# A language-model block on one core: projections a full step further ahead of the scores, a fifth buffer of values, and one buffer for the rests of q and k

## The chip, the core and the metric

The kernel runs on one core of one Trainium2 chip. The metric is the device time of one execution in microseconds (us), lower is better. The kernel before takes 623.44 us (median of three executions, 623.02 to 623.56).

## The reference

4096 tokens (32 rows of 128) of width 256 are looked up in a table, pass through causal attention with 16 heads of width 16, and then through a top-1 mixture of 8 experts (256 to 1024 to 256, GELU) with a capacity per expert. Each half takes a normalised input and is added to `h`.

```python
h = take(L0_tok_weight, x, axis=0)                       # (32, 128, 256)
n = layernorm(h)
q, k, v = (einsum('hkd,bsd->bhsk', w, n) for w in (q_w, k_w, v_w))
scores = where(causal, einsum('bhqk,bhsk->bhqs', q, k) / 4, -inf)
h = h + einsum('hdv,bhsv->bsd', o_w, einsum('bhqs,bhsk->bhqk', softmax(scores), v))
n = layernorm(h)
probs = softmax(n @ wg);  top1 = argmax(probs)           # 8 experts, slots in order of tokens
y = gelu(slots_of(n) @ W1 + b1) @ W2 + b2                # erf GELU
h = h + where(valid, y[slot], 0) * probs[top1]
```

## The kernel before

`attention_phase` handles the 32 rows in 16 groups of two (`NG` = 16, `GB` = 2); `expert_phase` then handles the 8 experts one after the other, bound by TensorE all along. The change touches the attention phase alone.

Attention is written as one loop of steps (line 257) that every engine runs through in its own queue, in order; semaphores alone tie the queues together. Each step `i` is cut into 8 places `s` (0 to 7). In step `i` a group `g = i` is projected: TensorE turns the normalised rows `xn` (line 767), ScalarE copies them as `xth`, VectorE makes the low part `xtl`, TensorE projects q at place 1, k at place 2 and v at place 7 (line 570, 12 matmuls of 256 columns for each). `turn4(bM0, xn)` for the next group stands at place 7 too.

Scores are needed with float32 accuracy from bfloat16 matmuls, so q and k are each split in three bfloat16 parts. For q: ScalarE writes the first part (`first_part`, line 456), VectorE the rest `qr` (`rest_of`, line 810), ScalarE the second part (line 461), GpSimd the third from `qr` (line 407). The same follows for k, with `kr` and line 410. The SP queue writes the parts to memory (lines 309 and 312) and reads them back stacked by head (`stacks`, line 301) into `qs` and `ks`, which have four buffers (`RING` = 4).

The scores, whose order is set by the three lags at line 267, come in 8 units for each group. A first pass (S, lines 599 and 602) only gives maxima (VectorE, `maxima`, line 796; a unit of TensorE waits for the maxima of the unit two before, as there are two banks). The maxima are turned (`pe_mT`, line 659), negated by ScalarE (`nm`, line 494), and sent by a DMA into a row of `qs`. A second pass (C, line 616) gives the shifted scores, ScalarE takes the exponent (line 442), GpSimd masks it (line 400), and TensorE multiplies it with the values `va` (PV, line 715). `va` is written by ScalarE at the end of each step (line 510).

Behind that come, group by group, one step after the other: `on` turned and copied into `oth` (line 465), the output projection and the residual, the second norm, routing (`route`, `place`) and the writes to the slots by GpSimd (line 366). GpSimd also gathers the token rows (`gather`, line 371): groups 0 to 2 ahead of the steps, then two groups in each step at places 6 and 7, two indirect DMAs for a group.

Statistics of the next group (`stats1`, line 755 to 762) stand on VectorE behind `maxima(4)`, its norm (`norm1`, line 767) behind `maxima(5)`; between them GpSimd raises the variance to the power -0.5 (line 414). SP also blanks the slots in six writes (line 323, steps 0 to 5) and loads the first experts' weights (steps 7 to 10). `idle_work` (line 529) is matmuls whose result nobody reads; they stand in the table `FILL`, and 14 of them stand ahead of the turn of group 1.

The lags of before, with `UNITS` = 8, mean: S of group g starts in step g+1 at place 4, C in step g+2 at place 7, PV in step g+3 at place 1.

## Time and profile before

| | |
|---|---|
| median of three executions | 623.44 us |
| the profiled execution | 626.09 us |
| its span in the profile | 624.4 us |
| TensorE (PE) busy | 576.3 us, 92% |
| VectorE (DVE) busy | 419.6 us, 67% |
| ScalarE (ACT) busy | 338.8 us, 54% |
| GpSimd (POOL) busy | 258.3 us, 41% |
| attention phase | up to about 357 us |
| expert phase | about 357 us to the end |

PE stands for TensorE's matmuls, PEld for its weight loads, which overlap them. An engine's busy share is a mean over both phases. The page also gives TensorE's granted clock for 40 equal slices of 15.6 us, in tenths: 9897999 and then 9 for nearly all the rest, so it is below full speed for a part of the second slice (15.6 to 31.2 us) and of the fourth (46.8 to 62.4 us). The profile's times run from the start of the span. A timeline row gives start, duration, engine, line and operation, output and input, and in brackets the idle time ahead of it with what ended it; rows of the same kind that follow one another are merged (x2, x4), with the time from first start to last end. Matmuls overlap, so their durations don't add up: one projection matmul starts every 0.12 us.

### The profile page before, as it was taken

The page shows a single profiled execution, that of the slowest core. Times are in us where ns is not written, and L with a number is a line of the kernel's source. Part 1 is how long each engine was busy: PE and PEld are TensorE (multiplying, and loading weights), DVE is VectorE, ACT ScalarE, POOL GpSimd, SP SyncE. Part 2 cuts the span into 40 slices and gives each one's busy share as a digit, 9 for nine tenths or more (in the row PEclk, how much of TensorE's full clock was granted, in tenths as well). Part 3 has the DMA queues.
Part 4 walks back from the last instruction along what each step waited for, and adds up shares of the span by engine and source line. Part 5 has one row for each costly group of instructions (what it writes and reads, how often), then busy time and mean ns, then how long its engine had stood idle before and what let it go on. Part 6 is the DMA issues. An engine that isn't in the chain of part 4 may idle for free. (4 is left out here: it accounts for less than half of the span.)

```text
span 624.4 us, 14332 instructions
## 1 busy us (share of the span) xinstructions
PE 576.3 (92%) x5311; PEld 498.5 (80%) x5371; DVE 419.6 (67%) x1073; ACT 338.8 (54%) x708; POOL 258.3 (41%) x316
## 2 busy tenths in 40 slices
PE   6778899989999999999898799999999999999993
PEld 3466677877877877787665369999999999999993
DVE  6255678988898888888766266565656575757531
ACT  2233555555555556555462168585858585858550
POOL 5445777765556655565563200404030403040303
PEclk9897999999999999999999999999999999999997
DMA  4678777546786644556111132151515151511101
GB/s 124 202 245 282 239 224 227 160 147 225 230 252 212 194 149 135 157 161 222 35 36 69 45 115 98 35 180 39 179 35 180 33 180 35 177 36 45 33 2 32
DMA packets 42581, 84.39 MB, mean 135 GB/s; under 512 B 6822, under 2 KB 32987, under 8 KB 38864
## 3 DMA queue, kind: packets, MB, share of 16 engines
q1 hardware_dynamic: 35600, 70.66, 35.6%
q0 software_dynamic: 6144, 12.67, 6.4%
q8 instruction: 44, 0.72, 0.5%
q14 instruction: 25, 0.20, 0.1%
q10 hardware_dynamic: 768, 0.13, 0.1%
HBM read 52.64 MB, written 31.74 MB: 135 GB/s over the span
## 5 line engine op out<-in xcount | busy, mean ns | idle before, releaser
L1009 POOL DMA_INDIRECT out_dram<-ys,xs x48 | 50.1, 1045 | 218.6 <-DVE ys L1206 209.1
L400 POOL TENSOR_SCALAR_AFFINE_SELECT pt<-pt 128x512 f32<-128x512 f32 x128 | 81.9, 640 | 86.0 <-ACT pt L442 84.5
L442 ACT ACTIVATE pt<-C 128x512 f32<-128x512 f32 x128 | 76.5, 598 | 72.1 <-PE C L616 68.1
L1219 DVE TENSOR_TENSOR hl<-gl,hh 128x324 fp32r<-128x324 f32 x128 | 63.3, 495 | 38.7 <-ACT hh L1049 34.1
L796 DVE TENSOR_REDUCE mx<-S 128x4 f32<-128x512 f32 x128 | 86.7, 681 | 4.0 <-PE S L602 2.2
L1049 ACT ACTIVATE hh<-gl 128x324 fp32r<-128x324 f32 x128 | 61.7, 491 | 0.0
L602 PE MATMUL S<-ks,qs 96*128 96x128 bf16 x512 | 50.2, 220 | 8.6 <-issue 6.6
L715 PE MATMUL PV<-pt,va 128*32 128x128 f32 x1024 | 54.1, 284 | 1.6 <-ACT os L449 0.8
L602 PEld LDWEIGHTS S<-ks,qs 96*128 96x128 bf16 x512 | 40.1, 98 | 15.7 <-issue 0.6
L616 PE MATMUL C<-qs,ks 97*128 97x128 bf16 x512 | 50.3, 220 | 1.0 <-DMA qs<-nm 1.0
L1206 DVE SCALAR_TENSOR_TENSOR ys<-C,xs 108x256 f32<-108x256 f32 x48 | 21.8, 481 | 40.1 <-PE C L1099 36.9
L1168 DVE TENSOR_TENSOR wel<-w_raw,weh 128x512 fp32r<-128x512 f32 x64 | 41.0, 684 | 9.4 <-ACT weh L1024 9.4
L1055 ACT ACTIVATE gl<-S,biases 128x324 f32<-128x324 f32 x64 | 34.7, 544 | 16.0 <-PE S L1133 11.8
L1024 ACT ACTIVATE weh<-w_raw 128x512 fp32r<-128x512 f32 x64 | 36.9, 645 | 10.5 <-PEq L159 10.5
L1133 PE MATMUL S<-xh,weh 128*128 128x324 f32 x128 | 41.1, 321 | 0.2 <-DVE xl L1182 0.2
L570 PE MATMUL M<-xth,wh 128*128 128x256 f32 x128 | 38.6, 301 | 2.7 <-DVE xtl L803 2.1
L1150 PE MATMUL M<-hh,weh 128*128 128x324 f32 x128 | 41.0, 321 | 0.0
L1150 PE MATMUL PV<-hh,weh 128*128 128x324 f32 x128 | 40.3, 315 | 0.0
L1133 PE MATMUL C<-xh,weh 128*128 128x324 f32 x128 | 40.2, 314 | 0.0
L1150 PE MATMUL M<-hl,weh 128*128 128x324 f32 x128 | 40.0, 312 | 0.0
L1150 PE MATMUL PV<-hl,weh 128*128 128x324 f32 x128 | 40.0, 312 | 0.0
L1133 PE MATMUL C<-xl,weh 128*128 128x324 f32 x128 | 40.0, 312 | 0.0
(157 smaller groups left out, 1706.8 us busy)
## 6 DMA issues: line engine op xcount, KB each, us to landing
w_raw<-in_L_ffn_W_dram SPq DMA_DIRECT2D x16, 1024.0 KB, 8.7
qs<-q_parts SPq DMA_DIRECT2D x48, 256.0 KB
ks<-k_parts SPq DMA_DIRECT2D x48, 256.0 KB
q_parts<-qp SPq DMA_DIRECT2D x16, 384.0 KB, 2.4
k_parts<-kp SPq DMA_DIRECT2D x16, 384.0 KB
rows_of_slots<-w_raw SPq DMA_DIRECT2D x6, 877.5 KB
xs<-rows_of_slots SPq DMA_DIRECT2D x8, 658.1 KB
out_dram<-h SPq DMA_DIRECT2D x16, 256.0 KB
```

Of the source, the lines that this page charges most:

```text
L400: pool.affine_select(out=buf[:, :, :], in_=buf[:, :, :], compare_op=ALU.is_ge, fill=0.0, base=0, pattern=[[0, 4], [1, S]], channel_multipl ...
L442: act.activation(pt[u % 4][:, :, :], bC[u % 2][:, :].rearrange("p (j t) -> p j t", j=4), ACT.Exp, scale=SCALE).then_inc(a_exp, 1)
L602: last = pe.matmul(dst[:, j * S:(j + 1) * S], qs[g.slot][0:KS_ROWS, hh, b * S:(b + 1) * S], ks[g.slot][0:KS_ROWS, hh, b * S:(b + 1) * S], ...
L616: last = pe.matmul(bC[u % 2][:, j * S:(j + 1) * S], ks[g.slot][:, hh, b * S:(b + 1) * S], qs[g.slot][:, hh, b * S:(b + 1) * S], start=True ...
L715: last = pe.matmul(bPV[32 * j:32 * j + 32, (u % QUADS) * S:(u % QUADS + 1) * S], va[g.slot][:, b, hh, :], pt[u % 4][:, j, :], start=True, ...
L796: dve.tensor_reduce(mx[g.slot][:, 4 * (u % QUADS):4 * (u % QUADS) + 4, u // QUADS], bS[u % 2][:, :].rearrange("p (j t) -> p j t", j=4), AX ...
L1009: pool.indirect_dma_start(out=outf, out_offset=bass.IndirectOffsetOnAxis(ap=xs[e.slot][:, j, D + 3:D + 4].bitcast(U32), axis=0), in_=ys[j] ...
L1049: act.activation(hh[:, f, cols], gl[u % 4][:, :], ACT.Copy).then_inc(a_hh, 1)
L1133: last = pe.matmul(up_bank[u % 4][:, 0:NH], w1[a][:, k, f * P:(f + 1) * P], xt[b][:, k, half * NH:(half + 1) * NH], start=(m == 0), stop=( ...
L1150: last = pe.matmul(down_bank[v % 2][:, 0:NH], w2[a][:, c, d * P:(d + 1) * P], ht[b][:, c, half * NH:(half + 1) * NH], start=(m == 0), stop ...
L1168: dve.tensor_tensor(wl[q][:, c * PC:(c + 1) * PC], raw[q][:, c * PC:(c + 1) * PC], wh[q][:, c * PC:(c + 1) * PC].bitcast(F32), ALU.subtrac ...
L1219: dve.tensor_tensor(hl[:, f, cols], gl[u % 4][:, :], hh[:, f, cols].bitcast(F32), ALU.subtract).then_inc(v_hl, 1)
```

## The change

The three lags grow by 8 places, so that S, C, PV and all that follows a group come one step later after its projection; there are 23 steps for 22. The places within a step stay. `va` gets a fifth buffer. `qr` and `kr` become one buffer `qkr`: the rest of q now waits for GpSimd's third part of k of the group before (`p_k3`), the rest of k for GpSimd's third part of q of the same group (`p_q3`). SP waits for the C pass of four groups before (`pe_C`) ahead of the stacked reads and no longer ahead of the writes of the parts. The blanking writes and the weight loads come one step later. In steps 0 and 1 the statistics and norm of the next group stand right behind `xtl` on VectorE, and GpSimd's power for them at place 0. The 14 matmuls of idle work ahead of group 1's turn are gone, and `FILL` has five at (1, 1), five at (2, 1) and eight at (2, 4) for six at (1, 1) and eight at (1, 4); its later entries move with the steps. The diff, cut where only the step's number in a `group(n, i - k)` or a `back(k)` grows by one:

```diff
--- before.py
+++ after.py
-AHEAD = 6
+AHEAD = 7
...
-        qr = sb("qr", [P, KC, GT], F32)
-        kr = sb("kr", [P, KC, GT], F32)
+        qr = kr = sb("qkr", [P, KC, GT], F32)
...
-        va = [sb(f"va{i}", [P, GB, H, 2 * DK], F32) for i in range(RING)]
+        va = [sb(f"va{i}", [P, GB, H, 2 * DK], F32) for i in range(RING + 1)]
...
-        S_LAG, C_LAG, PV_LAG = UNITS + 4, 2 * UNITS + 7, 3 * UNITS + 1
+        S_LAG, C_LAG, PV_LAG = 2 * UNITS + 4, 3 * UNITS + 7, 4 * UNITS + 1
...
@@ block.sync, step
-                    hold(sp, pe_C, g.back(RING - 1).times(UNITS))
                     hold(sp, p_q3, g.times(1, 1))
...
                 if g:
+                    hold(sp, pe_C, g.back(RING - 1).times(UNITS))
                     hold(sp, d_qw, g.times(16, 16))
                     stacks(qparts[g.slot], qs[g.slot], Q_PAIRS, d_q[g.slot])
...
-                if i < BLANKS:
-                    if i == 0:
+                if 1 <= i <= BLANKS:
+                    if i == 1:
                         sp.wait_ge(v_blank, 2)
...
-                if i == BLANKS + 1:
+                if i == BLANKS + 2:
                     sp.wait_ge(d_init, 16 * BLANKS)
-                if BLANKS < i <= BLANKS + 4:
-                    e, half = divmod(i - BLANKS - 1, 2)
+                if BLANKS + 1 < i <= BLANKS + 5:
+                    e, half = divmod(i - BLANKS - 2, 2)
...
-                g = group(n, i - 6)
+                g = group(n, i - 7)
...
@@ block.gpsimd, step
                     g = group(n, i + 1)
-                    if g and s == 5:
+                    if g and s == (0 if i < 2 else 5):
                         wait(pool, v_ve1, g.times(1, 1))
                         pool.tensor_tensor(rs1[:, :], ve1[:, :], halfneg[:, 0:GB], ALU.pow).then_inc(p_rs1, 1)
...
@@ block.scalar, step
-                g0, g2, g3, g4, g5, g6 = (group(n, i - k) for k in (0, 2, 3, 4, 5, 6))
+                g0, g2, g3, g4, g5, g6 = (group(n, i - k) for k in (0, 3, 4, 5, 6, 7))
...
-                    wait(act, pe_PV, g0.back(RING - 1).times(UNITS))
-                    act.activation(va[g0.slot][:, :, :, 0:DK].rearrange("p b h d -> p (b h) d"),
+                    wait(act, pe_PV, g0.back(RING).times(UNITS))
+                    act.activation(va[g0.off % (RING + 1)][:, :, :, 0:DK].rearrange("p b h d -> p (b h) d"),
...
@@ block.tensor
-            FILL = {(1, 1): 6, (1, 4): 8, (NG + 3, 1): 2, (NG + 3, 3): 3, (NG + 3, 5): 6, (NG + 3, 6): 3,
-                    (NG + 4, 1): 4, (NG + 4, 5): 4, (NG + 4, 6): 3, (NG + 5, 1): 4}
+            FILL = {(1, 1): 5, (2, 1): 5, (2, 4): 8, (NG + 4, 1): 2, (NG + 4, 3): 3, (NG + 4, 5): 6, (NG + 4, 6): 3,
+                    (NG + 5, 1): 4, (NG + 5, 5): 4, (NG + 5, 6): 3, (NG + 6, 1): 4}
...
                     g = group(n, i + 1)
                     if g and s == 7:
                         wait(pe, v_xn, g.times(1, 1))
-                        if g.off == 1:
-                            idle_work(bPV, 14)
                         wait(pe, v_qr, g.times(1))
-                        wait(pe, v_on, g.back(4).times(GB, 1))
+                        wait(pe, v_on, g.back(5).times(GB, 1))
                         turn4(bM0, xn).then_inc(pe_T, 1)
...
@@ block.vector
-            for i in range(RING):
+            for i in range(RING + 1):
                 last = dve.memset(va[i][:, :, :, DK:2 * DK], 1.0)
...
-                def rest_of(g, src, parts, rest, first_done, third_done, rest_done):
+                def rest_of(g, src, parts, rest, first_done, third_done, ahead, rest_done):
...
-                    wait(dve, third_done, g.times(1))
+                    wait(dve, third_done, g.times(1, ahead))
...
-                g0, g3, g4, g5, g6, nxt = (group(n, i - k) for k in (0, 3, 4, 5, 6, -1))
+                g0, g3, g4, g5, g6, nxt = (group(n, i - k) for k in (0, 4, 5, 6, 7, -1))
                 if g0:
                     low_part(g0, xtl, bM0, xth, a_xth, v_xtl)
+                if i < 2:
+                    stats1(nxt)
+                    norm1(nxt)
                 maxima(0)
...
-                    rest_of(g0, bM0, qp, qr, a_q1, p_q3, v_qr)
+                    rest_of(g0, bM0, qp, qr, a_q1, p_k3, 0, v_qr)
...
-                    rest_of(g0, bM2, kp, kr, a_k1, p_k3, v_kr)
+                    rest_of(g0, bM2, kp, kr, a_k1, p_q3, 1, v_kr)
...
-                if nxt:
+                if nxt and i > 1:
                     stats1(nxt)
...
-                if nxt:
+                if nxt and i > 1:
                     norm1(nxt)
```

## Rows read from the trace of the kernel before

**Rows 1.** Chain that ended last, in time: start us, us, what
```profile
356.96 4.77 DMA xs<-rows_of_slots
```

**Rows 2.** Timeline of ScalarE, copies into `oth`: start us, us, engine, line, operation
```profile
263.49 0.59 ACT L465 ACTIVATE oth<-M 128x512 fp32r<-128x512 f32 x1
...
281.75 0.59 ACT L465 ACTIVATE oth<-M 128x512 fp32r<-128x512 f32 x1
...
297.38 0.60 ACT L465 ACTIVATE oth<-M 128x512 fp32r<-128x512 f32 x1 [0.54 <-PE M L522]
...
312.31 0.60 ACT L465 ACTIVATE oth<-M 128x512 fp32r<-128x512 f32 x1 [0.71 <-PE M L522]
```

**Rows 3.** Windows: us, busy us of PE, PEld, DVE, ACT, POOL, clock, DMA
```profile
255.00:273.30 18.30, 17.66 (x222) 14.53 (x220) 16.23 (x47) 10.36 (x22) 10.92 (x15) 1.00 0.52 159
...
48.00:51.40 3.40, 1.74 (x16) 0.98 (x16) 3.08 (x10) 0.27 (x1) 2.69 (x3) 0.96 0.77 268
```

**Rows 4.** Timeline of ScalarE, copies into `xth` of groups 1 and 2
```profile
28.18 0.60 ACT L465 ACTIVATE xth<-M 128x512 fp32r<-128x512 f32 x1 [7.75 <-PE M L522]
...
40.08 0.59 ACT L465 ACTIVATE xth<-M 128x512 fp32r<-128x512 f32 x1
```

**Rows 5.** Windows, line 570 alone: us, busy PE, PEld, clock, DMA share, GB/s
```profile
37.85:39.35 1.50, 1.45 (x12) 1.47 (x12) 1.00 0.93 277
52.20:54.93 2.73, 2.69 (x12) 2.65 (x12) 0.50 0.82 240
```

**Rows 6.** Groups by line: xcount, busy us, mean ns, idle before, releaser
```profile
L734 DVE MEMSET va<- 128x512 f32 x4 | 1.9, 485 | 0.2
```

**Rows 7.** Timeline of VectorE, steps 0 to 2; in brackets the idle time before
```profile
13.56 0.68 DVE L803 TENSOR_TENSOR xtl<-M,xth 128x512 fp32r<-128x512 f32 x1
16.72 0.69 DVE L810 TENSOR_TENSOR qr<-M,qp 128x512 f32<-128x512 f32 x1 [2.48 <-ACT qp L456]
18.59 0.69 DVE L810 TENSOR_TENSOR kr<-M,kp 128x512 f32<-128x512 f32 x1 [1.18 <-ACT kp L456]
...
33.86 0.69 DVE L810 TENSOR_TENSOR kr<-M,kp 128x512 f32<-128x512 f32 x1 [1.18 <-ACT kp L456]
34.99 0.69 DVE L796 TENSOR_REDUCE mx<-S 128x4 f32<-128x512 f32 x1 [0.43 <-PE S L602]
...
48.37 0.74 DVE L755 BATCH_NORM_STATS2 st<-h 128x6 f32<-128x256 f32 x2
...
50.44 0.80 DVE L767 TENSOR_SCALAR xn<-h,mv,rs 128x256 f32<-128x256 f32 x2 [0.25 <-POOL rs L414]
```

**Rows 8.** Timeline of ScalarE, step 0
```profile
17.44 0.63 ACT L461 ACTIVATE qp<-qr 128x512 bf16<-128x512 f32 x1 [0.76 <-DVE qr L810]
...
19.32 0.63 ACT L461 ACTIVATE kp<-kr 128x512 bf16<-128x512 f32 x1 [0.76 <-DVE kr L810]
19.86 0.58 ACT L510 ACTIVATE va<-M 128x512 f32<-128x512 f32 x1
```

**Rows 9.** Timeline of GpSimd, step 0, and one power operation
```profile
18.16 1.16 POOL L407 TENSOR_TENSOR qp<-qr,qp 128x512 bf16<-128x512 f32 x1 [5.02 <-ACT qp L461]
20.03 1.16 POOL L410 TENSOR_TENSOR kp<-kr,kp 128x512 bf16<-128x512 f32 x1 [0.71 <-ACT kp L461]
...
22.19 1.16 POOL L375 DMA_INDIRECT h<-in_L_tok_weight_dram,idt  x1 [0.19 <-issue]
...
26.16 0.95 POOL L375 DMA_INDIRECT h<-in_L_tok_weight_dram,idt  x1 [0.30 <-issue]
...
49.68 0.73 POOL L414 TENSOR_TENSOR rs<-ve,halfneg 128x2 f32<-128x2 f32 x1 [0.53 <-DVE ve L762]
```

**Rows 10.** Timeline of all engines, a full step
```profile
188.26 1.16 POOL L407 TENSOR_TENSOR qp<-qr,qp 128x512 bf16<-128x512 f32 x1
...
189.50 0.69 DVE L810 TENSOR_TENSOR kr<-M,kp 128x512 f32<-128x512 f32 x1 [1.09 <-ACT kp L456]
```

**Rows 11.** Timeline of TensorE, step 2
```profile
46.87 0.38 PE L599 MATMUL S<-maskb,identb 128*128 128x512 bf16 x1 [1.26 <-DMA ks<-k_parts]
```

More of the change, by code:

```diff
@@ L418, in step @@
                         pool.tensor_tensor(mv2[:, :, 1], ve2[:, :], halfneg[:, 0:GB], ALU.pow).then_inc(p_rs2, 1)
-                    g = group(n, i - 6)
+                    g = group(n, i - 7)
                     if g and s in (4, 6):
@@ L619, in step @@
                         last.then_inc(pe_C, 1)
-                    g = group(n, i - 4)
+                    g = group(n, i - 5)
                     if g and s == 2:
                         wait(pe, v_h1, g.times(1))
-                        wait(pe, a_V, g.times(1, 4) if group(n, i - 1) else NG)
+                        wait(pe, a_V, g.times(1, 5) if group(n, i - 1) else NG)
                         turn_values(bM1, g, 1)
@@ L633, in step @@
                     if g and s == 2:
-                        wait(pe, a_nm, g.back(3).times(1, 1))
-                        wait(pe, v_base, g.back(6).times(1, 2))
+                        wait(pe, a_nm, g.back(4).times(1, 1))
+                        wait(pe, v_base, g.back(7).times(1, 2))
                         project(bM2, 1).then_inc(pe_K, 1)
                     if g and s == 7:
-                        wait(pe, v_h1, g.back(4).times(1, 1))
+                        wait(pe, v_h1, g.back(5).times(1, 1))
                         wait(pe, a_V, g.times(1))
@@ L668, in step @@
                         last.then_inc(pe_O, 1)
-                    g = group(n, i - 5)
+                    g = group(n, i - 6)
                     if g and s == 5:
@@ L672, in step @@
                         wait(pe, v_base, g.times(1, 1))
-                        wait(pe, a_nm, g.times(1, 4) if group(n, i - 2) else NG)
+                        wait(pe, a_nm, g.times(1, 4) if group(n, i - 3) else NG)
                         turn4(bM2, xn2).then_inc(pe_x2T, 1)
@@ L681, in step @@
                         last.then_inc(pe_lg, 1)
-                    g = group(n, i - 6)
+                    g = group(n, i - 7)
                     if g and s == 1:
@@ L697, in step @@
                         project(bM0, 0).then_inc(pe_Q, 1)
-                    g = group(n, i - 3)
+                    g = group(n, i - 4)
                     if g and s == 6:
-                        wait(pe, a_q1, g.times(1, 4) if group(n, i) else NG)
-                        wait(pe, v_qr, g.times(1, 4) if group(n, i) else NG)
+                        wait(pe, a_q1, g.times(1, 5) if group(n, i) else NG)
+                        wait(pe, v_qr, g.times(1, 5) if group(n, i) else NG)
                         wait(pe, v_on, g.times(GB, -1))
@@ L715, in step @@
                             last = pe.matmul(bPV[32 * j:32 * j + 32, (u % QUADS) * S:(u % QUADS + 1) * S],
-                                             va[g.slot][:, b, hh, :], pt[u % 4][:, j, :], start=True, stop=True)
+                                             va[g.off % (RING + 1)][:, b, hh, :], pt[u % 4][:, j, :], start=True, stop=True)
                         last.then_inc(pe_PV, 1)
```

12 lines of the change are left out of this document (6 added, 6 removed).

## The prediction

> **What bounds the kernel now.** I began with the chain of work that ended last, in order of time: its first long piece is the load of the experts' rows at 356.96, and all behind it is the expert phase, which isn't touched by this change [rows 1]. That phase follows attention directly, so whatever moves the end of attention moves the total one for one. I then read the attention phase as a row of steps.
>
> A full step costs 18.26 us, from one copy into `oth` (263.49) to the next (281.75). When only the last projection of values is left the interval is 15.63, and with no projection at all 14.93 [rows 2]. The step from 255.0 to 273.3 shows TensorE busy for 17.66 of 18.30 us [rows 3]: full steps are bound by TensorE. The first steps aren't. Step 1 has its `xth` copy at 28.18 and step 2 at 40.08 [rows 4], only 11.9 apart and not full of work; there each engine waits for a chain that runs through all of them. TensorE's clock suffers too: it worked 1.74 us between 48.0 and 51.4 [rows 3], and the twelve projection matmuls from 52.20 on were granted 0.50 of the clock, the 1.2 GHz level [rows 5].
>
> **What the change does to the order.** Call P(k) the projection work of group k and R(j) all else of old step j. Old step k held P(k)+R(k); new step k holds P(k)+R(k-1). There are 23 steps for 22, but the work is the same. Inside a full step nothing changes its place, so I cost these at nothing. The total is: what a second step of bare projections costs at the front, plus what the new waits cost in the ramp, minus what one step less with projections gives at the end.
>
> **The end.** Old: 18.26, 15.63, 14.93 for the three intervals between the `oth` copies of R(14), R(15), R(16), R(17). New: the first already has only the last values (15.63), the other two have none (14.93 each), if R(15) alone lasts as R(16) alone. Gain: 48.82 - 45.49 = 3.33 us. If just the one step sheds 18.26 - 15.63, it is 2.6; I take 3.3, as the kernel's order says.
>
> **A fifth value buffer** adds one fill of 485 ns to VectorE's start, whose four fills stand ahead of all its later work in its queue [rows 6]. I take 0.5; nothing, if VectorE waits there for a gather anyway. The buffer itself buys nothing: no row shows the copy into `va` waiting for PV.
>
> **The extra step at the front.** In new step 0, `stats1` and `norm1` of group 1 stand ahead of the rest of q. `xtl` starts at 13.56 and takes 0.68; statistics to the start of the norm are 50.44 - 48.37 = 2.07, the norm 0.80 [rows 7]. Rest of q: 13.56 + 0.68 + 2.07 + 0.80 = 17.1, against 16.72 now. Then second part of q 0.72 later (17.44 - 16.72), 17.8 [rows 7, 8]; third part of q on GpSimd 0.72 later (18.16 - 17.44), 18.55, for 1.16, to 19.7 [rows 9]. Here the shared buffer bites: the rest of k may only be written once GpSimd has read the rest of q, so it starts at 19.75, not 0.73 us before that end as now (18.59 against 18.16 + 1.16). Second part of k 0.73 later (19.32 - 18.59), 20.5, copy of values 0.54 later (19.86 - 19.32), 21.0, next `xth` copy when that one is nearly done (0.58 long; 0.5): step 1 starts at 21.5, against 28.18 now, because the norm of group 1 no longer stands behind everything and 14 filling matmuls are gone.
>
> GpSimd: third part of k 0.71 after the second (20.03 - 19.32), 21.2 to 22.35. Now the gathers of groups 3 and 4, four instructions on its queue, from first start to last start 26.16 - 22.19 = 3.97, plus 0.95 [rows 9]: 22.55 to 27.5. In new step 1 the power for group 2's norm is GpSimd's first operation, so it stands behind these gathers. VectorE waits for it, and the rest of q of group 1 is queued behind that norm. Power 0.73 [rows 9]: 28.2; norm 0.80: 29.05. Rest of q 29.05, second part 29.8, third part 30.5 to 31.65, rest of k 31.7, second part of k 32.4, values 33.0, `xth` 33.5. So new step 2 starts 33.5 - 28.2 = 5.3 us after old step 1 did, and both hold R(1).
>
> **The next steps.** In new step 1 the third part of k ends at 33.1 + 1.16 = 34.3 and the gathers of groups 5 and 6 run to 34.5 + 4.9 = 39.4. The third part of q of group 2 can't start before. Old step 1 had the rest of k at 33.86, 5.7 after its `xth`: it would be at 39.15; now 39.4 + 1.16 = 40.6, so 1.45 later. The first maximum stood at 34.99, with 0.43 of idle time before it [rows 7]; of the 1.45, 1.0 reaches it. Scores then wait for maxima through two banks: +1.0. In old step 2, as in 0 and 1, the rest of k started some 0.7 before the end of the third part of q (the row of step 0 stands for the three), so the new wait adds 0.75, and the later maxima of that step are behind it: +0.75. In full steps the third part ends at 188.26 + 1.16 = 189.42 and the rest of k starts at 189.50, held by ScalarE's first part [rows 10]: the new wait fits with 0.08 to spare, cost nothing, up to 0.3 a step if it slips. The stacks' DMA wait before the scores (1.26 at 46.87) [rows 11] goes, but VectorE reaches these maxima only after the rest of k, so it buys nothing on the chain.
>
> **The clock.** From about 27.3 (values of group 1 done) to 35 TensorE has only four transposes and five fills, 1.7 us of work in 8. That is thinner than old 48.0 to 51.4, behind which the clock was at half. I expect the 1.2 GHz level when Q of group 2 starts. Twelve projection matmuls took 1.45 us at 2.4 GHz and 2.69 at 1.2 [rows 5]: +1.25. The third part of q would have started 5.25 after `xth` (the rest of k less 0.43), 38.7; with 1.25 it is 40.0 against the 39.4 of the gathers: +0.6. Between 0 and 2.5: if K runs slowly too, the same 1.25 again.
> The Trainium skill, "TensorE: Matmul & The Clock Gate", section "HAM oscillation — how this bites in real kernels", says that each long TensorE wait makes the work after it start cold. By that rule every lull of the ramp costs again, and the term would be nearer 2.5 than 0.6, the total 630.2; [rows 3, 5] agree with it for the one lull that they show.
>
> **Sum.** +5.3 +0.5 +1.0 +0.75 +0.6 -3.3 = +4.85 us. The profiled execution, 626.09 us with a span of 624.4, would be 630.9 with a span of 629.2. The median shown is 623.44, which is 2.65 below the profiled one; there the forecast is **628.3 us**, 0.8% slower.
>
> **Rivals.**
> 1. Not slower: the ramp gives back its stalls. Place: R(2) and R(3), old 44.6 to 58.3. TensorE waited 1.26 for the stacks [rows 11]; 48.0 to 51.4 has 1.74 busy of 3.4; the twelve matmuls behind it lost 1.25 to the clock, and as much again, by my estimate, is lost until it is back. If stacks that lie ready a step early keep TensorE dense there, 1.3 + 1.7 + 2.5 = 5.5 go, and the 0.75 with them: 628.3 - 6.25 = 622.0. It decides from 4.85 us on. For it: these waits are real. Against: two of the three hang on VectorE's order, which the change makes longer. Chance 0.15, with 0.1 more that it gives about half, 625.2.
> 2. The clock stays low: K, the eight fills and the scores of R(1) too. 1.25 for K and about as much for the rest instead of 0.6: 628.3 + 1.9 + 0.3 = 630.5. For it: the lull is the longest of the ramp. Chance 0.15.
> 3. Full steps change. Their idle time is 18.30 - 17.66 = 0.64 [rows 3]; 13 of them. If stacks issued later take half of it away, 628.3 - 4.2 = 624.1; if the new wait slips by 0.3 in each, 632.2. No row speaks for either. Chance 0.05 each.
>
> **How the numbers follow.** Forecast 0.5, its own range 626 to 630. Slower: 0.5 + 0.15 + 0.05, and half of the halfway case, 0.75. Within 0.2% (1.25 us), which is about what a measurement of this kernel can tell from no change: the other half and 624.1, 0.1. Faster: 0.15. The range goes from 622.5, just above rival 1, to 631.5, above rival 2: 0.15 below, some 0.05 above.
>
> **What would show it.** Right: `xth` copies at 21.5 and 33.5 to 34; VectorE idle for 3 to 4 us before the norm of group 2, released by GpSimd's power; the rest of k released by GpSimd's third part in the first four groups and by ScalarE later; full steps of 18.2 to 18.3; intervals of 15.6, 14.9, 14.9 at the end; expert phase from about 361.8. Wrong: a first maximum of group 0 before 39; full steps off 18.25 by over 0.1; no saved projection step at the end; a low clock that is gone from R(2).

## The result, and the profile after

The kernel after takes 632.11 us (median of four executions, 631.17 to 633.03) against 623.5 us for the kernel before beside it on the same chip: a ratio of 1.0117, 95% interval 1.0093 to 1.0141. This ratio isn't the quotient of the two medians, which is 1.0138. The kernel is slower than the forecast of 628.3 us under both: by its median it lies 0.6 us beyond the top of the range (631.5), by the ratio (1.0117 times 623.44, 630.7 us) just inside. Its profiled execution took 632.45 us with a span of 630.6, against 626.09 and 624.4. So 6.2 us of difference can be read from the two spans; the medians lie 8.6 apart because the profiled execution of before was 2.6 us above its own median, and that of after 0.3.

The copies into `xth` (start us, us, engine, line, operation, idle time ahead and what ended it), groups 0 to 4 and then 7 and 8, to be held against [rows 4]:

```profile
12.62 0.60 ACT L464 ACTIVATE xth<-M 128x512 fp32r<-128x512 f32 x1 [1.68 <-PE M L521]
...
21.61 0.59 ACT L464 ACTIVATE xth<-M 128x512 fp32r<-128x512 f32 x1
...
33.26 0.59 ACT L464 ACTIVATE xth<-M 128x512 fp32r<-128x512 f32 x1
...
46.65 0.59 ACT L464 ACTIVATE xth<-M 128x512 fp32r<-128x512 f32 x1
...
66.67 0.60 ACT L464 ACTIVATE xth<-M 128x512 fp32r<-128x512 f32 x1 [0.19 <-PE M L521]
...
116.69 0.59 ACT L464 ACTIVATE xth<-M 128x512 fp32r<-128x512 f32 x1
...
135.06 0.59 ACT L464 ACTIVATE xth<-M 128x512 fp32r<-128x512 f32 x1
```

Steps 0 and 1 end where the working put them (21.6 and 33.3, forecast 21.5 and 33.5). The step that sticks out is the fourth, 46.65 to 66.67: 20.0 us, for one that has the work of old step 2, 40.08 to 56.04. The four copies into `oth` that answer to [rows 2]:

```profile
271.29 0.59 ACT L464 ACTIVATE oth<-M 128x512 fp32r<-128x512 f32 x1
286.76 0.60 ACT L464 ACTIVATE oth<-M 128x512 fp32r<-128x512 f32 x1 [0.35 <-PE M L521]
301.67 0.60 ACT L464 ACTIVATE oth<-M 128x512 fp32r<-128x512 f32 x1 [0.72 <-PE M L521]
316.58 0.60 ACT L464 ACTIVATE oth<-M 128x512 fp32r<-128x512 f32 x1 [0.71 <-PE M L521]
```

Intervals of 15.47, 14.91 and 14.91: the end behaves as forecast. With every event of after held against the one of before that has the same scores to do, the difference runs like this:

| event | before | after | difference | step of it |
|---|---|---|---|---|
| scores of group 0 start (`xth` of old step 1, new step 2) | 28.18 | 33.26 | +5.1 | +5.1 |
| next `xth` | 40.08 | 46.65 | +6.6 | +1.5 |
| maxima of group 0 negated (`nm`) | 48.23 | 54.80 | +6.6 | 0 |
| next `xth` | 56.04 | 66.67 | +10.6 | +4.1 |
| three steps on | 107.91 | 116.69 | +8.8 | -1.8 |
| `oth` of group 10 (before) and its like | 263.49 | 271.29 | +7.8 | -1.0 |
| last of the four `oth` above | 312.31 | 316.58 | +4.3 | -3.5 |
| experts' rows are loaded | 356.96 | 362.44 | +5.5 | +1.2 |
| span | 624.4 | 630.6 | +6.2 | +0.7 |

**The step that wasn't forecast.** ScalarE, around the maxima of group 0:

```profile
54.80 0.27 ACT L493 ACTIVATE nm<-M 32x128 bf16<-32x128 f32 x1 [0.31 <-PE M L656]
55.09 0.60 ACTq L497 DMA_DIRECT2D qs<-nm  x1
63.22 0.60 ACT L441 ACTIVATE pt<-C 128x512 f32<-128x512 f32 x1 [8.16 <-PE C L615]
```

and the first C on TensorE:

```profile
62.58 0.61 PE L615 MATMUL C<-qs,ks 97*128 97x128 bf16 x4 [4.73 <-DMA qs<-nm]
```

In before, ScalarE's issue and TensorE's first C:

```profile
48.53 0.60 ACTq L498 DMA_DIRECT2D qs<-nm  x1
```

```profile
51.87 0.61 PE L616 MATMUL C<-qs,ks 97*128 97x128 bf16 x4 [1.01 <-DMA qs<-nm]
```

A transfer of 8 KB held TensorE until 7.5 us after its issue (62.58 - 55.09); before it was 3.3 us (51.87 - 48.53). The windows of after around it (us; busy us of PE, PEld, DVE, ACT, POOL; clock; DMA share; GB/s):

```profile
49.00:52.50 3.50, 3.50 (x34) 2.99 (x32) 1.45 (x3) 1.78 (x3) 0.93 (x2) 1.00 1.01 316
52.50:56.00 3.50, 1.33 (x14) 0.75 (x11) 2.80 (x8) 0.90 (x2) 1.68 (x2) 1.00 1.01 260
56.00:59.50 3.50, 1.04 (x5) 0.50 (x5) 2.69 (x6) 0.00 (x0) 2.77 (x3) 0.53 0.95 334
59.50:63.00 3.50, 0.42 (x5) 0.43 (x5) 0.00 (x0) 0.00 (x0) 0.06 (x1) 0.50 0.76 264
63.00:66.50 3.50, 3.50 (x19) 3.46 (x18) 0.00 (x0) 1.19 (x2) 2.15 (x3) 0.51 0.86 246
```

The DMA engines were full when the row was issued and stayed so (share 1.01 and 0.95); in before they were full just ahead of it too (0.96 from 45.0 to 48.5), but the stretch 48.0 to 51.4 had 0.77 [rows 3]. From issue to matmul the mean share was 0.90 in after and 0.67 in before. What filled them stands on SP's queue (the rows are issues):

```profile
49.03 2.17 SPq L300 DMA_DIRECT2D qs<-q_parts  x3
51.24 1.86 SPq L300 DMA_DIRECT2D ks<-k_parts  x3
53.15 0.58 SPq L322 DMA_DIRECT2D rows_of_slots<-w_raw  x1
53.77 0.43 SPq L307 DMA_DIRECT2D q_parts<-qp  x1
```

By the page these are six reads of 256 KB, a blanking write of 877.5 KB and a write of 384 KB: 2.8 MB in the 6.1 us ahead of the row. In before SP issued 384 KB in the 6.1 us ahead of its row, since there the reads went out at 37.05, right behind the writes of the parts, and the blanking write at 40.82. In after the parts of q of group 2 were issued at 40.58 and SP waited for them to land, the last 5.9 us with nothing else to do, before it issued the reads at 49.03; so the reads themselves came late, just ahead of the row. The clock was 0.50 to 0.53 from 56.0 to 66.5, through the wait and the first projections behind it.

**Where the ramp agreed.** GpSimd's four gathers and what stands behind them, and VectorE's wait for it:

```profile
22.62 1.02 POOL L374 DMA_INDIRECT h<-in_L_tok_weight_dram,idt  x1 [0.16 <-issue]
...
26.45 0.95 POOL L374 DMA_INDIRECT h<-in_L_tok_weight_dram,idt  x1 [0.30 <-issue]
27.42 0.73 POOL L413 TENSOR_TENSOR rs<-ve,halfneg 128x2 f32<-128x2 f32 x1
...
28.19 0.73 DVE L764 TENSOR_SCALAR xn<-h,mv,rs 128x256 f32<-128x256 f32 x2 [4.12 <-POOL rs L413]
```

and the shared buffer, whose rest of k follows the end of the third part of q (39.09 + 1.16 = 40.25, then 40.36), the third part itself having stood behind the next four gathers:

```profile
38.11 0.96 POOL L374 DMA_INDIRECT h<-in_L_tok_weight_dram,idt  x1 [0.30 <-issue]
39.09 1.16 POOL L406 TENSOR_TENSOR qp<-qkr,qp 128x512 bf16<-128x512 f32 x1
...
40.36 0.69 DVE L807 TENSOR_TENSOR qkr<-M,kp 128x512 f32<-128x512 f32 x1 [2.17 <-POOL qp L406]
41.55 0.69 DVE L793 TENSOR_REDUCE mx<-S 128x4 f32<-128x512 f32 x1 [0.50 <-PE S L601]
```

The first maximum came at 41.55, 6.6 later than in before [rows 7].

### The profile page after: what moved, and what is told of

Same layout as the page of the kernel before. It is cut to its first block and busy times, and to the rows that moved or that the text cites. A ratio compares the mean times of both kernels' runs of the same rounds, so it can differ in the third digit from the quotient of the medians.

```text
span 630.6 us, 14372 instructions
## 1 busy us (share of the span) xinstructions
PE 586.4 (93%) x5361; PEld 499.7 (79%) x5361; DVE 416.5 (66%) x1074; ACT 346.4 (55%) x708; POOL 258.3 (41%) x316
## 5 line engine op out<-in xcount | busy, mean ns | idle before, releaser
L1049 ACT ACTIVATE hh<-gl 128x324 fp32r<-128x324 f32 x128 | 59.2, 469 | 0.0
L598 PE MATMUL S<-maskb,identb 128*128 128x512 bf16 x128 | 50.0, 391 | 2.6 <-DVE mx L793 2.6
## 6 DMA issues: line engine op xcount, KB each, us to landing
rows_of_slots<-w_raw SPq DMA_DIRECT2D x6, 877.5 KB, 8.1
```

Source lines behind the costliest of these rows:

```text
L598: pe.matmul(dst[:, :], identb[:, :], maskb[:, :, :], start=True, stop=False)
L1049: act.activation(hh[:, f, cols], gl[u % 4][:, :], ACT.Copy).then_inc(a_hh, 1)
```

## The experiments

Ratios are to the kernel before on the same chip, with 95% intervals; they aren't exactly the quotients of the medians (`e3_one_gather` has 1.0104 for a quotient of 1.0143). The runs were made on three chips: the first four kernels beside a before of 626.66 us, the next four beside 627.38, the last four beside 624.84 and 624.76. The kernel after was timed on the second of them alone, so what an edit is worth against after is read from the traces and from ratios, and a few tenths of a per cent between chips say nothing. Theory A says that the unforecast time is traffic on the DMA engines around the row of maxima. Its rivals are the queues of VectorE and GpSimd (gathers, shared buffer), and chance in a single execution. Each edit has one traced execution.

**Does a trace of before repeat?** `e1_before_again` is the kernel before, unchanged.

> The kernel before once more, unchanged, for a second trace of it. The profiled execution of before (626.09 us) lies 2.6 us above the median of its unprofiled ones (623.5), that of the changed kernel (632.45) at its median. Theory A: the two stalls of ScalarE that end with no releaser in step 6 of before's trace (1.6 and 2.4 us, after which full steps run 1.4 us later than those of the changed kernel) are accidents of that execution; then this trace has a span near 622 and the oth copies of step 8 on come 1 to 2 us earlier than before's. Theory B: they belong to the kernel; then the span is 624.4 again and the ledger of the two traces (6.2 us) is all there is.

625.81 us, span 624.1. In old step 6, before had an interval of 20.05 us between `xth` copies that the forecast passed over, with 2.4 us of idle time on ScalarE that no semaphore of another engine ended:

```profile
107.91 0.59 ACT L465 ACTIVATE xth<-M 128x512 fp32r<-128x512 f32 x1
...
127.46 0.60 ACT L510 ACTIVATE va<-M 128x512 f32<-128x512 f32 x1 [2.39 <-remote]
127.96 0.59 ACT L465 ACTIVATE xth<-M 128x512 fp32r<-128x512 f32 x1
```

This execution had it again, 107.41 to 127.09, 19.7 us. So it wasn't the accident of one trace. After's step there took 18.4 (116.69 to 135.06), and before's next one was 0.7 shorter than after's (17.6 for 18.2): 1.7 less 0.7 is the -1.0 of the table.

**Blanks moved out of the ramp.** `e2_blank_late` is after with the six blanking writes in steps 4 to 6, two each, for one each in steps 1 to 6.

```diff
-                if 1 <= i <= BLANKS:
-                    if i == 1:
+                if 4 <= i <= 6:
+                    if i == 4:
                         sp.wait_ge(v_blank, 2)
-                    sp.dma_start(...[:, i - 1], blank).then_inc(d_init, 16)
+                    for a in (2 * i - 8, 2 * i - 7):
+                        sp.dma_start(...[:, a], blank).then_inc(d_init, 16)
```

> The changed kernel with its six blanking writes (877 KB each) two at a time in steps 4, 5 and 6 in place of one in each of steps 1 to 6. In the changed kernel the 8 KB DMA of the first row of maxima, issued at 55.1, released the C pass only some 7 us later, against 3.3 us in before, with the DMA engines at 0.95 to 1.02 of their time from 24.5 to 59.5. Theory traffic: it waits behind the stacked reads and the blanks; with 1.75 MB (some 6 us at 290 GB/s) less ahead of it the wait falls by 3 to 5 us, and the total by 3 to 5 us, to 627 to 629. Theory queues (only the order on VectorE and GpSimd counts): no change, 632.

629.57 us, ratio 1.0047 (1.0019 to 1.0074). The row was issued at 56.04 and C ran at 58.65, with no DMA wait left on TensorE:

```profile
58.65 0.61 PE L616 MATMUL C<-qs,ks 97*128 97x128 bf16 x4
```

```profile
56.00:59.50 3.50, 2.38 (x19) 1.67 (x17) 3.19 (x10) 0.21 (x2) 2.48 (x4) 0.63 0.65 228
```

2.6 us for 7.5, and a DMA share of 0.65 for 0.95 in the same window. Over the 2.6 us themselves the share was still 0.84; what differs more is the bulk that SP issued in the 6.1 us ahead of the row, 0.9 MB for 2.8. The next `xth` stood at 62.81 for 66.67, though the one before it was 0.6 later than in after. Theory A holds for this wait. In the total it is worth less than the 3 to 5 us expected: the span is 627.9 for 630.6, or for 629.2 in the second execution of after below, and the interval of this ratio overlaps that of after's (1.0047 to 1.0086).

**One group gathered in a step, for two.** `e3_one_gather` is after with the gathers at place 6 alone.

```diff
-                    if isinstance(n, int) and gathers and s in (6, 7):
+                    if isinstance(n, int) and gathers and s == 6:
```

> The changed kernel with one group gathered in each step in place of two, so that GpSimd's power for group 2's norm stands behind two indirect DMAs and not four. Theory queues: the norm of group 2 (28.19) comes 2.5 us earlier, the xth copy of group 2 at 30.8 in place of 33.26, the third part of q of group 2 no longer waits for gathers, together 3 to 3.5 us less: 629. Theory traffic: the step comes earlier, but the row of maxima waits that much longer for the same bytes, less the 0.5 MB of two groups not yet gathered (under 2 us): 630.5 to 632.

635.61 us, ratio 1.0104 (1.0061 to 1.0147). Two gathers fewer on GpSimd's queue brought step 2 forward, 31.39 for 33.26, but step 3 came at 46.96, no earlier than after's 46.65. The gathers then last until new step 13, and full steps in which GpSimd writes slots as well rose from 18.25 to 19.1 us:

```profile
135.51 0.60 ACT L464 ACTIVATE xth<-M 128x512 fp32r<-128x512 f32 x1 [0.84 <-remote]
...
154.55 0.60 ACT L464 ACTIVATE xth<-M 128x512 fp32r<-128x512 f32 x1 [0.16 <-remote]
...
173.71 0.60 ACT L464 ACTIVATE xth<-M 128x512 fp32r<-128x512 f32 x1 [0.18 <-remote]
```

From 116.10 to 230.87, six steps took 5.3 us more than at 18.25; that is the loss, and the row took 5.6 us (55.41 to 60.99). Why a gather beside slot writes costs this is open: the idle time is ScalarE's, ended by nothing the trace names, the same mark as in old step 6.

**Two rests again.** `e4_two_rests` is after with `qr` and `kr` apart, and their waits as in before. To find room, `nm` has two buffers and three small inputs lie in a free part of another buffer.

```diff
-        qr = kr = sb("qkr", [P, KC, GT], F32)
+        qr, kr = sb("qr", [P, KC, GT], F32), sb("kr", [P, KC, GT], F32)
```

> The changed kernel with two buffers for the rests of q and k again and the waits of before on them; the room comes from two nm buffers in place of four and from x, its float copy and the raw biases in a part of the first weights' buffer that is free at that time. The shared buffer alone held the rest of k by 1.0 us in each of steps 0 and 1, 0.75 to 1.4 in steps 2 and 3, and by nothing from step 4 on. Theory queues: 1 us earlier in step 1, 2 in step 2, together 2 to 3 us less: 629.5. Theory traffic: what comes earlier waits longer at the row of maxima: 631 to 632.5.

629.46 us, ratio 1.0039 (1.0016 to 1.0062). `xth` at 20.74, 31.58 and 44.80 for 21.61, 33.26 and 46.65: the shared buffer costs 0.9 us in the first step, 1.7 by the second and 1.9 by the third. The row's wait stayed, issued at 52.69, C at 59.67:

```profile
59.67 0.61 PE L615 MATMUL C<-qs,ks 97*128 97x128 bf16 x4 [4.65 <-DMA qs<-nm]
```

7.0 us, at a DMA share of 0.98. Two causes, then: queues ahead of the row, and traffic under it. As with the late blanks, the gain in the medians isn't told apart from none: the interval of the ratio overlaps that of after's.

**After, on another chip.** `e5_after_again` is after unchanged.

> The changed kernel once more, on one chip with the next three, so that they can be set against it and not only against before. Theory window: the low stretch of TensorE's clock in the drain (near 339, then 1.2 us lost between two oth copies) and the one at the start of the expert phase (near 363) are in all four traces of kernels with the new order and in none of the two of before; so they belong to the order and appear again. Theory chance: they go by where the execution happens to fall, and are missing or elsewhere here. The ramp (xth copies at 12.6, 21.6, 33.3, 46.6, first C unit after 62) repeats within 0.5 us until the third copy under both.

631.42 us (631.23 to 632.67), ratio 1.0067 (1.0047 to 1.0086). After is as fast here as on its first chip; before isn't (627.38 against 623.5). The size of the loss thus differs from one measurement to the other, 0.7 to 1.2%, its sign doesn't; whether the chip or the time makes the difference isn't shown.

The ramp repeated up to the third copy (33.23) and not behind it: the fourth came at 48.33 for 46.65, since TensorE's clock fell again, and the twelve matmuls for the values of group 2, from 44.64 on, started 0.21 us apart for 0.12:

```profile
43.50:47.00 3.50, 2.79 (x16) 2.68 (x17) 2.58 (x6) 0.00 (x0) 2.87 (x4) 0.66 0.96 360
```

The row then took 5.0 us (56.80 to 61.82), and the step 17.3 (48.33 to 65.64) for 15.7 in the second execution of before (40.55 to 56.26). So this pair has +3.2 where the table has +1.5, +1.6 where it has +4.1, and +0.2 where it has -1.8. The ramp's loss is much the same, but not where it falls. In the window in which after had its clock at 0.89, this execution had 1.00:

```profile
334.00:341.00 7.00, 4.72 (x48) 2.53 (x48) 5.03 (x26) 1.30 (x3) 3.20 (x4) 1.00 0.09 32
```

Its experts' rows were loaded at 360.94 for 362.44. The +1.2 of the drain thus isn't a property of the change. The spans of the two second executions differ by 5.1 us (629.2 and 624.1).

**Gathers spread.** `e6_gathers_split` is after with one group gathered in step 0 for two, the next at place 1 of step 1, behind the power, and two groups in each later step.

```diff
-                    if isinstance(n, int) and gathers and s in (6, 7):
+                    if isinstance(n, int) and gathers and (i, s) != (0, 7) and (
+                            s in (6, 7) if i != 1 else s in (1, 6)):
```

> The changed kernel with the gathers of steps 0 and 1 at other places: group 3 alone in step 0, group 4 in step 1 at place 1, behind the power for group 2's norm, group 5 at place 6; from step 2 on two in each step, up to step 6, so that none meets the writes of the slots. Theory queues: the norm of group 2 comes 2.5 us earlier (25.7), the xth copy of group 2 at 30.8, that of group 3 some 3 us earlier than 46.6; total 3 us under the changed kernel if nothing behind takes it up. Theory traffic: the first C unit waits for the row of maxima all the same; it starts at 60 to 62.5 and the total gains under 1.5 us. Against one gather a step this has no gathers in steps 7 to 12: full steps stay at 18.25, where they were 19.1.

632.02 us, ratio 1.0077 (1.0053 to 1.0101). Step 2 started at 31.07 and step 3 at 45.63, 2.2 and 1.0 earlier than in after. The row still took 4.8 us (54.64 to 59.44, mean share 1.00), and ScalarE waited 4.3 us for parts of q. The profiled execution was 1.1 us shorter than that of after on the same chip (630.10 for 631.23), but the median isn't, with executions from 630.1 to 633.4: a gain of some 1 us at most, which these four executions can't tell from none.

**All three together.** `e7_combined` has the edits of the second, fourth and sixth experiment.

> Late blanks, two rests and split gathers at once on the changed kernel. Theory: the three costs of the ramp lie one behind the other, and what one frees the traffic no longer takes. Each xth copy: group 1 at 20.7, group 2 at 29.2 (31.6 of two rests less 2.4), group 3 at 41.5, group 4 at 57 against 66.7; then 9 us under the changed kernel, about 622, at or a little under before (ratio 0.993 to 1.000). If the traffic of stacked reads alone binds the ramp, the first C unit stays over 56 and the ratio is over 1.003.

626.41 us, ratio 0.9983 (0.9964 to 1.0003). `xth` at 20.66, 29.05, 44.77 and 58.81: the ramp is 8 us shorter than after's. The first part of q of group 2 is now what waits, for a write that stands in the same traffic:

```profile
34.89 0.60 ACT L456 ACTIVATE qp<-M 128x512 bf16<-128x512 f32 x1 [5.25 <-DMA q_parts<-qp]
```

TensorE's clock fell too, to 0.55 in the window from 30.5 to 34.0, behind 2.33 us of waiting for `xtl`. It was busy for all of that window, so this wasn't idle time; the copy above waited for the DMA and not for TensorE.

**The early norm in the kernel before.** `e8_before_front` gives before the new front alone: statistics and norm of group 1 right behind `xtl`, the power at place 0, no 14 idle matmuls; no extra step.

```diff
-                    if g and s == 5:
+                    if g and s == (0 if i < 1 else 5):
...
                     low_part(g0, xtl, bM0, xth, a_xth, v_xtl)
+                if i < 1:
+                    stats1(nxt)
+                    norm1(nxt)
...
-                        if g.off == 1:
-                            idle_work(bPV, 14)
```

> The kernel before with the front part of the change alone: statistics and norm of group 1 behind xtl in step 0, the power at place 0, and without the 14 matmuls of idle work; lags, buffers and all else as before. Theory: the xth copy of group 1 comes at 20.7 in place of 28.2; its scores of group 0 then need the stacks, which land near 32 as now (third part of k ends at 21.2, the reads issued at 21.8 to 25.6), while the units would be ready at 27; so of the 7.5 us some 3 to 5 reach the first maxima (30 to 32 in place of 35) and the total: 619 to 621. Rival: the ramp is bound by the traffic of the stacks and the row of maxima lands as late as now, gain under 1 us.

627.70 us, ratio 1.0006 (0.9993 to 1.0019). Step 1 began at 20.43 for 28.18 and none of these 7.7 us was kept. The scores can't start before the stacks have landed, at 33.80 for 34.34 in before:

```profile
33.80 0.58 PE L599 MATMUL S<-maskb,identb 128*128 128x512 bf16 x1 [7.06 <-DMA ks<-k_parts]
```

That leaves 0.5 us, and the clock took more: it was 0.50 from 32.0 to 40.0, behind 7.06 us of waiting, and step 2 began at 41.77 for 40.08. The old ramp thus had 0.5 us to gain before the way of q and k through memory bound it. What the early norm would give with the clock kept up wasn't tried. In after the extra step stands over that wait, at its own price.

**A refilled ramp.** `e9_combined_fill` is the combined kernel with more idle matmuls in front of the places where it had been cold.

```diff
-            FILL = {(1, 1): 5, (2, 1): 5, (2, 4): 8,
+            FILL = {(1, 1): 5, (2, 1): 11, (2, 4): 6, (2, 6): 4, (2, 7): 5, (3, 6): 4, (3, 7): 4,
```

> The combined kernel (late blanks, two rests, split gathers) with more idle work in the ramp's lulls: 11 at (2, 1), 6 at (2, 4), 4 at (2, 6), 5 at (2, 7), 4 at (3, 6) and (3, 7), in place of 5 at (2, 1) and 8 at (2, 4). In its trace TensorE ran at 1.2 GHz from 30.5 to 33.9 and 40.8 to 44.2, where twelve projection matmuls take 2.7 us and not 1.45, after waits of 2.3 us for xtl and 1.0 and 1.3 us for maxima, which these fills occupy. Theory clock: the first two low stretches go, the xth copy of group 3 comes at 43 and not 44.8, the total is 1.5 to 2.5 us under the combined kernel, ratio 0.994 to 0.997. Theory traffic: the copy of the first part of q of group 2 waits for the DMA of the parts of group 1 (5.3 us, until 34.9) whatever the clock does; the fills gain under 0.5 us, ratio 0.997 to 0.999.

623.46 us, ratio 0.9979 (0.9962 to 0.9997) to before's 624.84: the best of all kernels here, and ahead of before by no more than a measurement can just tell. Its low stretches:

```profile
37.50:41.00 3.50, 1.21 (x7) 0.73 (x9) 2.71 (x8) 1.32 (x3) 2.40 (x3) 0.87 0.92 272
41.00:44.50 3.50, 3.50 (x20) 2.43 (x18) 2.45 (x5) 0.00 (x0) 2.74 (x3) 0.64 0.96 311
```

The stretch 30.5 to 34.0 is back at 1.00 from 0.55. The wait for the parts of q is still there, 5.44 us, until 35.72; and the `xth` copies of both kernels lie within 0.1 us of each other at groups 4 and 5 (58.73 and 73.82 for 58.81 and 73.91); from group 6 on this one is 1.3 us ahead (90.62 for 91.87). Between the ratios 0.9983 and 0.9979 there is nothing to choose. Group 3's copy came at 45.38, where the theory of the clock had 43: the wait for the write decided there.

**Fewer steps with gathers, in before.** `e10_before_gathers` gathers a third group in step 0 of before, so that the gathers end a step earlier.

```diff
-                    if isinstance(n, int) and gathers and s in (6, 7):
+                    if isinstance(n, int) and gathers and (s in (6, 7) or (i, s) == (0, 5)):
```

> The kernel before, with three groups gathered in step 0, so that the gathers end in step 5 and not in step 6, in which the first writes of the slots are GpSimd's. Step 6 took 20.0 and 19.7 us in the two traces of before, against 18.25 for full steps; in the changed kernel, whose first slot writes come in step 7 without gathers, no step was over 18.5. Theory GpSimd: four indirect DMAs for gathers and two for slots in one step delay the masking of the last units, and so PV; without the meeting step 6 takes 18.3 to 18.6, total 1.2 to 1.6 us less. Rival: the steps' own first meeting with routing work costs the 1.5 us; no change (under 0.4).

625.16 us, ratio 1.0000 (0.9984 to 1.0016). Its trace has step 6 at 18.4 us and a span of 620.9, but the medians don't follow. Either the stall isn't in every execution, or something else is given back; the experiment doesn't tell which.

**The shared buffer in before.** `e11_before_shared` has that one edit, with its waits.

```diff
-        qr = sb("qr", [P, KC, GT], F32)
-        kr = sb("kr", [P, KC, GT], F32)
+        qr = kr = sb("qkr", [P, KC, GT], F32)
```

> The kernel before with the one buffer for both rests, and nothing else of the change: its lags, gathers, blanks and fills. Theory: the rest of k waits for GpSimd's third part of q, 0.75 us in each of steps 0 to 2, 0.3 in step 3, nothing from step 4 on (0.06 to 0.08 us to spare). In step 1 the fills at (1, 4) and the stacks cover it in part, in step 2 the maxima stand behind it: total 0.7 to 1.5 us more than before; full steps 18.25. Rival: with so little to spare the wait slips in full steps too, 18.35 or more, and the total rises by 2 to 4 us.

626.29 us, ratio 1.0023 (1.0007 to 1.0039), which is 1.4 us. `xth` at 29.00 and 41.39 for 28.18 and 40.08 [rows 4]; the full steps stayed at 18.26, from 144.0 on. This is the new wait's price by itself, and all that the trace shows of it is in the ramp, in steps 0 and 1: from `xth` to `nm` step 2 took 8.15 us (41.39 to 49.54), as in before. Step 6 took 18.4 us here too (107.16 to 125.57), though its gathers and slot writes are those of before. That speaks against gathers as the whole cause of the 20.05.

**Stacked reads a step later.** `e12_late_stacks` is the refilled kernel with SP issuing the reads of a group in the step after its writes, so that the parts of the next group go first.

```diff
                 if g:
...
+                g = group(n, i - 1)
+                if g:
                     hold(sp, pe_C, g.back(RING - 1).times(UNITS))
```

> The combined kernel with fills, and SP now issues the stacked reads of group g-1 in step g behind the writes of the parts of group g, which the longer lag allows. In the combined kernel's traces the first part of q of group 2 waited 5.4 us (to 35.7) for the DMA that writes the parts of group 1, issued at 28.4 behind 1.5 MB of stacked reads of group 0. Theory traffic order: that DMA lands near 31, the copy starts at 32.2; the reads of group 0 are issued at 30.3 to 34 and land near 38, so the first maximum stands at 38.5 to 39 as now, but the rest of k no longer holds the maxima behind it, and the reads no longer stand ahead of the next parts: xth of group 3 at 43.5 and of group 4 at 57 in place of 45.4 and 58.7, total 1.5 to 2 us less, ratio 0.994 to 0.996. Rival, traffic as a sum: the same bytes have to pass before the scores, only in another order; the copy comes earlier and the first scores later by as much, ratio 0.997 to 0.999.

627.63 us, ratio 1.0040 (1.0025 to 1.0055), against 0.9979 without the edit. The part of q that had waited ran at 32.26 for 35.72, as the order says. But the reads, issued from 30.38 to 34.4, now held the scores:

```profile
41.90 0.58 PE L600 MATMUL S<-maskb,identb 128*128 128x512 bf16 x1 [6.92 <-DMA ks<-k_parts]
```

```profile
35.50:39.00 3.50, 0.00 (x0) 0.00 (x0) 0.00 (x0) 0.62 (x1) 1.15 (x1) 0.77 1.03 239
```

TensorE did nothing for a whole window while the DMA engines were full, and step 3 came at 50.55 for 45.38. The row of maxima took 2.6 us here, for 3.2, but the wait for the stacks outweighed it. This order moved the wait and didn't shorten it; taking bytes out of the ramp (the late blanks) did.

**All executions together.** The wait from the issue of the first row of maxima to its matmul can be read in fourteen traces. The bulk that SP issued in the 6.1 us ahead of the row is added up from its issue rows and the sizes of the page (rows that stand merged are spread evenly, so it is an estimate). With the blanks out of the ramp, or in the order of before, it was 0.4 to 1.2 MB, the wait 2.6 to 3.7 us (nine traces). In the five traces with after's blanks and lags it was 2.0, 2.0, 2.3, 2.4 and 2.8 MB, the wait 4.8, 5.0, 5.6, 7.0 and 7.5 us.

## Why the prediction was right in sign and short in size

**Full steps: right.** After's `oth` copies lie 18.24 apart (253.05 to 271.29), against 18.26 [rows 2]. The shared buffer's 0.08 us of room [rows 10] held.

**The end: right.** 3.5 us gained for 3.3; the interval with the last values was 15.47 for the 15.63 that I took over.

**The extra step at the front: right.** +5.1 for +5.3 and +0.5. The steps in between came out within 0.3 us, as did GpSimd's power behind four gathers (27.42 for 27.5) and VectorE's wait there (4.12 for 3 to 4). The memset was sized too high: the first `xth` moved from 12.31 to 12.62, 0.3 us. The rest of k was released by GpSimd's third part in five groups (the last at 73.51), one more than I said.

**Third part of q behind the gathers, and the clock: right together.** +1.5 for 1.0 + 0.6. The clock did fall where I expected it, when Q of group 2 starts:

```profile
31.50:35.00 3.50, 0.28 (x2) 0.31 (x3) 1.38 (x2) 1.60 (x3) 1.89 (x2) 1.00 0.89 246
35.00:38.50 3.50, 3.50 (x21) 3.50 (x20) 0.69 (x1) 0.88 (x2) 2.59 (x4) 0.60 0.86 242
38.50:42.00 3.50, 3.45 (x23) 2.03 (x21) 1.15 (x2) 1.58 (x3) 1.94 (x3) 0.91 1.00 277
```

It came back within that step, so the rival with a clock that stays low through K and the scores didn't happen there. In the second execution of after it half did: 0.70 and 0.81 from 33.0 to 40.0, then 0.66 from 43.5 to 47.0, and +3.2 for these two terms together. So the size of this term changes from one execution to the next, and that 1.5 met 1.6 was in part luck. The 0.3 in rival 2's sum is worked out nowhere. The Trainium skill, "TensorE: Matmul & The Clock Gate", section "HAM oscillation — how this bites in real kernels", was named for each long wait making the next work cold. By that rule the term would have been nearer 2.5; less the 1.0 ahead of it, it was 0.5 in the first execution and 2.2 in the second. The lull from 56.0 to 63.0 agrees with the rule (0.50 to 0.53, and 0.51 for the 3.5 us of work behind it), but before had paid for the same lull with its twelve matmuls at 0.50 [rows 5], so the sum got nothing from it. In the drain the same work ran with and without a low clock in two executions of after.

**The 0.75 in R(2): the wait was there, the price wasn't.** From the rest of q to the rest of k it is 2.69 us in new step 3 (50.44 to 53.13) for 1.87 in old step 2, so the new wait added 0.8 as written. But the first part of q ran 3.2 us behind `xth` and not 4.0, and the step from `xth` at 46.65 to `nm` at 54.80 takes 8.15 us, as in before (40.08 to 48.23). The shared buffer alone, in before, shows the same exchange, 8.15 again. Without it, in new order, the step took 7.6 (44.80 to 52.40). What brought q forward in the two kernels with the shared buffer is open.

**The step that failed: "it buys nothing on the chain".** That sentence settled the DMAs of the ramp. The stacks' wait did go, as written, but I looked only at what a transfer ready in time could give, and at no transfer that might come too late. In new step 3 the stacks of group 2, a blanking write and the parts of the next group were issued within 6 us ahead of the row of maxima, the one transfer that TensorE waits for with nothing else to do. In before it already had a wait of 1.01 us (51.87), which I didn't list: the blanks and the stacks move by a step, and I costed neither against what stands beside them afterwards. Price: 4.1 us, of which the following steps gave back 1.8; in the second pair of executions 1.6, of which nothing came back. That the load is the cause is shown by the late blanks, 2.6 us for 7.5 and 5.0, and by the other traces: 2.6 to 3.2 us in the four kernels with late blanks, 4.8 to 7.5 in the five executions without them. It isn't the order on one queue, since the row is issued from ScalarE and the bulk from SP. The Trainium skill, "DMA: Bandwidth & Descriptors", section "Issuing engines are not separate DMA queues", says that DMAs of all issuing engines run on the same 16 engines and interleave. The 7.5 us of this row agree.

**Rival 1, the ramp gives back its stalls: fell,** and inverted. It took the stalls of R(2) and R(3) for lack of stacks, but the row of maxima was late by more than the stacks had been. With the blanks late, two rests and the gathers spread, the total was 626.41 to 627.38, near the rival's 1.4 us under before; but that kernel also lacks the shared buffer's cost and the gathers' wait, and its clock fell in the ramp, so whether the rival's mechanism gave any of it isn't shown.

**Rival 3, full steps change: didn't,** but the trace of before had one step of 20.05 us among those of 18.25 that I hadn't looked for. What makes it is open. It came again in the second execution of before and in the one with the new front (19.7 and 19.6) and was absent with a third group gathered early and with the shared buffer, and its absence in the trace with the early gather moved no median.

**The rest.** The drain's 1.2 us go with the low clock there and are chance, as the second execution shows. At the experts' start the window 362 to 369 had the clock at 0.76 in both executions of after; in before the like window, 357 to 364, had 1.00. With it go 0.7 us. It isn't the new order alone, since before with the new front had 0.78 from 355 to 362; why is open. The bridge from profile to median was a step of its own: adding 4.85 to 623.44 takes it that after's profiled execution too lies 2.65 above its median. It lay 0.34 above. Of the 3.8 us by which the forecast missed, 1.5 are the profiled executions (632.45 for 630.9) and 2.3 are this. That the two profiled executions came within 1.5 us of the sum, and the second pair within 0.3 (5.1 for 4.85), is luck: the row's wait was missing from the sum, and the steps behind the row, the 1.0 of old step 6, the 0.75 and a front that cost less than 5.8 made up for most of it.

## What to carry to other kernels

A pipeline that runs one stage further ahead pays a whole bare step at its start (11.7 us here, of which an earlier start gave back 6.6) and gets a step without that stage's work at its end (3.5 us): it pays only where full steps gain, and these didn't. Before such a change, list every small transfer that an engine waits for with nothing else to do, and what bulk will be issued just ahead of it in the new order. Where the DMA engines are full there, move bulk that nobody waits for (here the blanking writes) out of the ramp; a new order of the same bytes can be worse, as it was here (ratio 1.0040 for 0.9979).

## What the runs showed of the hardware

- From the issue of an 8 KB row to the matmul that waits for it took 2.6 to 3.7 us where the mean DMA share over that time was 0.55 to 0.84 (nine traces), and 4.8 to 7.5 where it was 0.90 to 1.00 (after twice, one gather, two rests, gathers spread). Within the second lot the wait goes with the bulk issued in the 6.1 us ahead (2.0 to 2.8 MB, an estimate) and not with the share: 7.5 us was at 0.90 and 4.8 at 1.00.
- The same matmuls of the same kernel, the values of group 2, started 0.12 us apart in one execution and 0.21 in the other (granted clock 0.66 from 43.5 to 47.0).
- Steps that hold gathers beside slot writes by GpSimd took 19.1 us for 18.25 in one kernel, by idle time on ScalarE that the trace lays to no engine; yet such a step ran in 18.4 in before with the shared buffer.
- The same kernel before took 623.5, 626.7, 627.4 and 624.8 us on the chips used, each at its own time, and after 632.1 and 631.4 on two of them. The loss of one kernel against the other was 1.2% on one chip and 0.7% on another (by the medians 1.4% and 0.6%).
